# A one-core decoder layer: the expert routing list inverted by one-hot matmuls, rows gathered by the experts, residual and layernorm done on the sorted tiles

## The chip, the cores and the metric

The kernel runs on one core of a Trainium2 chip. The metric is device time in microseconds (us), the median of several executions. The core has a matrix engine (TensorE, PE in the rows), a vector engine (VectorE, DVE), an activation engine (ScalarE, ACT) and GpSimd (POOL). SyncE (SP) issues most DMAs; indirect DMAs, whose row numbers come from a table in memory, are issued by POOL.

## The reference, cut to what matters

The input is 32 batches of 128 tokens with 128 features, in float32. Three blocks follow each other, each with a residual and a layernorm. The change touches what surrounds the third, a mixture of eight experts with one expert per token:

```
x = layernorm(x + attention(x))                 # 16 heads, two segments
x = layernorm(x + cross_retention(x, ctx))      # x is called x2 from here on
gate_scores = softmax(x @ Wg + bg)              # 8 experts
e = argmax(gate_scores); top = gate_scores[e]
y = (silu(x @ W1[e] + b1[e]) @ W2[e] + b2[e]) * top
x = layernorm(x + y)
```

## The kernel before, in words

The kernel is five phases, one behind the other, each a block with its own program for every engine; the next block starts when all engines, and the DMAs they wait for, are done with the last one. The phases are `attention_phase`, `retention_phase`, `gate_phase`, `expert_phase` and `finish_phase`. Tokens lie as `[P, B, D]`: 128 token positions on the partitions, 32 batches, 128 features. Loops over groups of `G` = 4 batches give `NG` = 8 steps.

The retention phase works by groups and, on SP, loads the expert weights W1, W2 and the bias b2 ahead (`preload`). It then fills the DRAM buffer `sorted_x` from the tile `padding`: zero rows, each with a number of a spare output row.

The gate phase normalises x2 (`x2_row`), computes the logits, the softmax, `top` and the one-hot `hot`. Each expert's tokens are to fill whole tiles of 128 rows, so there are up to `NT` = 32 + 8 - 1 = 39 tiles. Two matmuls on `hot` and a chain of small DVE operations give, for each token, its row in the sorted order (`place`), and for each tile its expert (`tile_expert`). POOL then scatters x2 with 32 indirect DMAs, one per batch, into `sorted_x` (line 1142), the token's own number beside its 128 features.

The expert phase loads `sorted_x` back in four pieces (`cuts`). It runs over the 39 tiles in a loop of pairs. For tile t: ACT copies it (`e_x`), PE turns it (`e_turn`, line 1327), DVE evacuates it (`e_xT`, line 1414). Each engine reads the tile's expert number into a register (`expert_of`), and DVE copies that expert's W1 (`w_cur`, line 1410), ACT its biases (`b_cur`, line 1374). PE makes the hidden layer (`h_bank`, line 1343), ACT applies Silu (`hT`, line 1392), PE makes the output one tile later (`y_bank`, line 1353), DVE adds b2 (`y`, line 1433), and POOL scatters the tile's rows back into token order in the DRAM buffer `y_rows` (line 1314), behind a small addition (`carrier`, line 1313).

The finish phase loads `y_rows` in eight pieces, adds `y * top` to x2 and takes the statistics (DVE, partly POOL), makes mean and scale for all 32 batches at once (`norm_dve`, `norm_act`, lines 123 to 157), normalises and stores.

## Time and profile before

| | |
|---|---|
| time, median of 3 runs | 903.24 us (900.38 to 904.02) |
| the profiled execution | 903.15 us, span 901.3 us |
| busy share of the span | PE 79%, DVE 67%, ACT 59%, POOL 57% |
| granted TensorE clock, mean | 0.899 of 2.4 GHz |
| HBM traffic | 67.42 MB read, 43.16 MB written |

The span runs from the first to the last instruction of the profiled execution. Attention ends and retention begins at about 602 us, the gate phase begins at 684.8, the experts at 771.0 and the finish phase at 869.7. In the rows below a number in square brackets is the engine's idle time ahead of the instruction with what ended it. SPq stands for a DMA issue on SP's queue. The granted clock has two levels: 1.00 is 2.4 GHz, 0.50 is 1.2 GHz; a value between is a mean over a stretch in which it changed.

### The profile page before, as it was taken

The numbers are of one execution on the slowest core, as the hardware profiler recorded it, in microseconds if no ns is written. First come the engines' busy times: TensorE is split into PE (matmuls) and PEld (weight loads), VectorE is DVE, ScalarE is ACT, GpSimd is POOL, SyncE is SP. The second block draws the span as 40 slices with busy tenths as digits, with TensorE's granted clock in tenths as the row PEclk, the third lists the DMA queues.
The fourth block names the chain that finished last, engine by engine and source line by source line (L and its number), as shares of the span: only waits on it lengthen the run. The fifth ranks groups of instructions, "written<-read, shape, count | busy, mean of one in ns | idle before, by whom it ended". The sixth has DMA issues, their size and how long they took to land. (4 is left out here: it accounts for less than half of the span.)

```text
span 901.3 us, 26782 instructions
## 1 busy us (share of the span) xinstructions
PE 712.1 (79%) x9501; PEld 597.7 (66%) x9502; DVE 605.1 (67%) x1217; ACT 528.7 (59%) x1119; POOL 513.4 (57%) x524
## 2 busy tenths in 40 slices
PE   4789999999999999999999999748994600599920
PEld 3577788788778778778778877645664500598920
DVE  4378788788788788878878878745885510244438
ACT  3677787788788778778778878321221100477720
POOL 2167667757757756766765775633431167266742
PEclk8799999999999999999999999967996555699975
DMA  7567767767667677676776776611093011400033
GB/s 239 117 179 200 187 170 205 176 163 215 171 161 216 172 172 199 178 183 177 197 180 170 209 171 162 160 32 36 25 284 51 0 39 53 124 32 29 32 108 93
DMA packets 122154, 127.72 MB, mean 142 GB/s; under 512 B 7424, under 2 KB 101920, under 8 KB 118032
## 3 DMA queue, kind: packets, MB, share of 16 engines
q1 hardware_dynamic: 119584, 122.17, 52.8%
q0 software_dynamic: 2544, 5.21, 1.7%
q8 instruction: 15, 0.25, 0.1%
q14 instruction: 11, 0.09, 0.0%
HBM read 67.42 MB, written 43.16 MB: 123 GB/s over the span
## 5 line engine op out<-in xcount | busy, mean ns | idle before, releaser
L328 POOL TENSOR_TENSOR lhs<-pos_qv,ungate 64x1024 f32<-64x1024 f32 x64 | 151.7, 2370 | 161.9 <-PE mix L495 151.2
L614 ACT ACTIVATE psT<-bank 128x512 f32<-128x512 f32 x128 | 72.6, 594 | 92.5 <-PE bank L484 92.5
L766 DVE TENSOR_TENSOR lhs<-mix,zg_all 64x512 f32<-64x512 f32 x128 | 88.2, 689 | 5.8 <-PE mix L467 1.9
L353 POOL TENSOR_TENSOR e_qk<-e_qk 128x512 f32<-128x512 f32 (+2 forms) x96 | 78.6, 819 | 20.1 <-DVE e_qk L707 15.1
L484 PE MATMUL bank<-const,ps 128*128 128x128 f32 x512 | 70.0, 280 | 21.7 <-POOL ps L343 21.5
L598 ACT ACTIVATE e_qk<-e_qk 128x512 f32<-128x512 f32 x128 | 82.3, 643 | 0.0
L721 DVE TENSOR_REDUCE s_max<-bank 128x8 f32<-128x512 f32 x64 | 44.2, 691 | 48.7 <-PE bank L453 47.8
L467 PEld LDWEIGHTS mix<-pos_qv 64*64 64x64 f32 (+1 forms) x2048 | 65.6, 137 | 13.7 <-issue 11.2
L484 PEld LDWEIGHTS bank<-const,ps 128*128 128x128 f32 x512 | 55.2, 142 | 27.9 <-issue 15.7
L574 ACT ACTIVATE qk_tok<-bank 128x512 f32<-128x512 f32 x128 | 73.2, 601 | 0.0
L603 ACT ACTIVATE qkT<-bank 128x512 f32<-128x512 f32 x128 | 71.2, 610 | 1.8 <-PE bank L430 1.0
L467 PE MATMUL mix<-pos_qv 64*64 64x64 f32 (+1 forms) x2048 | 72.2, 225 | 0.0
L495 PE MATMUL mix<-psT,lhs 128*64 128x64 f32 x2048 | 69.7, 229 | 3.0 <-DVE lhs L766 2.2
L495 PEld LDWEIGHTS mix<-psT,lhs 128*64 128x64 f32 x2048 | 65.3, 143 | 8.6 <-issue 8.6
L389 PE MATMUL bank<-w_k,x_cur 128*128 128x512 f32 x192 | 63.6, 442 | 7.5 <-ACT psT L614 7.5
L430 PE MATMUL bank<-const,qk_tok 128*128 128x128 f32 x512 | 67.2, 273 | 2.7 <-DVE e_qk L707 2.1
L1410 DVE COPY w_cur<-w 128x512 f32 x39 | 16.8, 431 | 77.3 <-issue 48.6
L512 PE MATMUL bank<-w_o,attT 128*128 128x128 f32 x512 | 65.2, 282 | 4.0 <-DVE attT L700 4.0
L512 PEld LDWEIGHTS bank<-w_o,attT 128*128 128x128 f32 x512 | 61.0, 195 | 10.7 <-ACT qkT L603 7.1
L430 PEld LDWEIGHTS bank<-const,qk_tok 128*128 128x128 f32 x512 | 59.4, 140 | 12.8 <-DVE e_qk L707 2.5
L343 POOL TENSOR_TENSOR ps<-s_exp,row_rec 128x512 f32<-128x512 f32 x64 | 65.4, 1042 | 0.0
L336 POOL TENSOR_TENSOR ps<-pos_qv,sq_rec 128x1024 f32<-128x1024 f32 x32 | 60.9, 1902 | 5.9 <-POOL lhs L328 4.8
(212 smaller groups left out, 1694.5 us busy)
## 6 DMA issues: line engine op xcount, KB each, us to landing
scratch_qv<-qv_out SPq DMA_DIRECT2D x32, 1024.0 KB, 5.7
pos_qv<-scratch_qv SPq DMA_DIRECT2D x64, 512.0 KB, 6.6
swapT<-qkT SPq DMA_DIRECT2D x64, 256.0 KB, 4.0
zg_all<-scratch_z SPq DMA_DIRECT2D x64, 256.0 KB, 3.8
sorted_x<-padding SPq DMA_DIRECT2D x1, 2515.5 KB, 18.5
r_all<-in_x_dram SPq DMA_DIRECT2D x4, 512.0 KB, 7.0
cx<-in_ctx_dram SPq DMA_DIRECT2D x8, 256.0 KB, 2.7
w<-in_L_ffn_W_dram SPq DMA_DIRECT2D x1, 2048.0 KB, 9.7
```

Of the source, the lines that this page charges most:

```text
L328: pool.tensor_tensor(lhs[0:L, 1 - n, :, :], pos_qv[s, :, DK:], ungate[s, :, :], ALU.mult).then_inc(vg_ready, 1)
L353: pool.tensor_tensor(dst, e_qk[:, 0:c, DK:], e_qk[:, c:2 * c, DK:], ALU.add).then_inc(k_summed, 1)
L430: last = pe.transpose(qk_bank[f][:, i * P:(i + 1) * P], qk_tok[:, 4 * f + i, :], cst("ident"))
L467: last = pe.matmul(mix[odd * DK:(odd + 1) * DK, h // 8, at:at + DK], pos_qv[0:k, h, 0:DK], pos_qv[0:k, h, DK:], start=True, stop=True)
L484: last = pe.transpose(turn_bank[f % 2][:, i * P:(i + 1) * P], ps[:, 4 * f + i, :], cst("ident"))
L495: last = pe.matmul(mix[odd * DK:(odd + 1) * DK, n, at:at + L], lhs[:, 1 - n, h, :], psT[:, h, n * L:(n + 1) * L], start=True, stop=True)
L512: last = pe.matmul(score_bank[1][:, 0:D], attT[:, c, :], w_o[:, c, :], start=(c == 0), stop=(c == C // 2 - 1))
L574: act.activation(qk_tok[:, 8 * hh:8 * hh + 8, slot * DK:(slot + 1) * DK], half_bank(bank, hh), ACT.Copy).then_inc(evac, 1)
L598: act.activation(e, e, ACT.Exp, scale=-1.0).then_inc(grown, 1)
L603: act.activation(qkT[:, :, 4 * f:4 * f + 4], qk_bank[f][:, :].rearrange("p (c s) -> p s c", c=4), ACT.Copy).then_inc(qkT_evac, 1)
L614: act.activation(psT[:, 4 * f:4 * f + 4, :], turn_bank[f % 2][:, :].rearrange("p (h s) -> p h s", h=4), ACT.Copy).then_inc(psT_evac, 1)
L766: dve.tensor_tensor(dst, mix[odd * DK:(odd + 1) * DK, g, :].rearrange("p (i n k) -> p i n k", n=SEG, i=4), zg_all[odd * DK:(odd + 1) * DK, ...
```

## The change

The padding of `sorted_x` in the retention phase, the 32 scatters of the gate phase and the whole finish phase are gone. The gate phase now makes the inverse list, which token lies at each row of each tile. `place` is split into tile (shift by 7) and row in the tile (the low 7 bits). For each batch two one-hot matrices, `in_row` (128x128) and `in_tile` (128x39, multiplied by the token's number + 1 on POOL), are multiplied on PE and summed over the 32 batches in one bank. From the sum come `token_of` (the number, with 0 for empty rows) and `row_to` (the same, with a number past the end for empty rows). Meanwhile SP stores x2 with `top` in its last column to the DRAM buffer `x2_rows`.

In the expert phase POOL gathers each tile from `x2_rows` by `token_of` with one indirect DMA, the first 16 (`AHEAD`) at once and the others four at a time. The loops are written out: every engine's program is straight-line code over 39 tiles. PE turns the gathered tile directly. DVE adds b2, then in two more operations per tile makes the residual (`y * top + x2`) and its statistics; per group of four tiles it does `norm` (mean and variance) and one tile later `scale_of` (scale and shift). Between these, POOL raises the variance to -0.5 (`raise_var`). ACT normalises tile t - 6 in its step t, in place of the copy `e_x`. POOL scatters the finished tile straight to the output by `row_to`, with a bounds check that leaves the empty rows out. The functions `stage_w1`, `evac`, `hidden` and `output` do what the loop bodies did before. The diff, cut to its core:

```diff
+EMPTY = 2.0 * P * B
+AHEAD = 16
...
             for target, source in preload:
                 sp.dma_start(target, source).then_inc(preloaded, 16)
-            sp.wait_ge(padded, 2)
-            sp.dma_start(sorted_x.rearrange("(t p) d -> p t d", p=P), padding[:, :, :]).then_inc(preloaded, 16)
-            sp.wait_ge(preloaded, 16 * (len(preload) + 1))
+            sp.wait_ge(preloaded, 16 * len(preload))
...
-            pool.memset(padding[:, :, :], 0.0).then_inc(padded, 1)
-            pool.wait_ge(padded, 1)
-            pool.tensor_copy(padding[:, :, D:].rearrange("p t o -> p (t o)"), cst("spare_row")).then_inc(padded, 1)
...
+            sp.wait_ge(x2_kept, NG)
+            sp.wait_ge(top_kept, 1)
+            sp.dma_start(x2_rows.rearrange("(b p) d -> p b d", p=P), x2_row[:, :, :]).then_inc(x2_stored, 16)
+            sp.wait_ge(x2_stored, 16)
...
+            for b in range(B):
+                if b % G == 0:
+                    pe.wait_ge(in_row_ready, b // G + 1)
+                if b % (B // 2) == 0:
+                    pe.wait_ge(in_tile_ready, b // (B // 2) + 1)
+                last = pe.matmul(list_bank[:, 0:NT], in_row[:, b, :], in_tile[:, b, :], start=(b == 0), stop=(b == B - 1))
+            last.then_inc(listed, 1)
...
+            act.wait_ge(top_ready, 1)
+            act.activation(x2_row[:, :, D:].rearrange("p b o -> p (b o)"), top[:, :], ACT.Copy).then_inc(top_kept, 1)
...
-            pool.tensor_copy(x2_row[:, :, D:].rearrange("p b o -> p (b o)"), cst("token_row")).then_inc(x2_kept, 1)
-            pool.wait_ge(x2_kept, NG + 1)
-            pool.wait_ge(placed, 1)
-            for b in range(B):
-                pool.indirect_dma_start(sorted_x, bass.IndirectOffsetOnAxis(ap=place[:, b:b + 1], axis=0),
-                                        x2_row[:, b, :], None).then_inc(scattered, 16)
-            pool.wait_ge(scattered, 16 * B)
+            for i in range(2):
+                half_b = slice(i * B // 2, (i + 1) * B // 2)
+                dims = [P, B // 2, NT]
+                pool.wait_ge(placed, i + 1)
+                pool.tensor_tensor(in_tile[:, half_b, :], in_tile[:, half_b, :],
+                                   cst("token_row")[:, half_b].unsqueeze(2).to_broadcast(dims), ALU.mult).then_inc(in_tile_ready, 1)
...
-            dve.tensor_copy(place[:, :], place_f[:, :]).then_inc(placed, 1)
-def expert_phase(nc, const, w1, w2, biases, tile_expert, sorted_x, y_rows):
+            dve.tensor_copy(place[:, :], place_f[:, :]).then_inc(done, 1)
+            dve.wait_ge(done, n + 13)
+            dve.tensor_scalar(tile_u[:, :], place[:, :], 7, None, ALU.logical_shift_right).then_inc(done, 1)
+            dve.tensor_scalar(row_u[:, :], place[:, :], P - 1, None, ALU.bitwise_and).then_inc(done, 1)
+            dve.wait_ge(done, n + 15)
+            dve.tensor_copy(tile_f[:, :], tile_u[:, :]).then_inc(done, 1)
+            dve.wait_ge(done, n + 15)
+            dve.tensor_copy(row_f[:, :], row_u[:, :]).then_inc(done, 1)
+            dve.wait_ge(done, n + 17)
+            for g in range(NG):
+                if g % (NG // 2) == 0:
+                    s = slice(G * g, G * g + B // 2)
+                    dims = [P, B // 2, NT]
+                    dve.tensor_tensor(in_tile[:, s, :], cst("tile_at").unsqueeze(1).to_broadcast(dims),
+                                      tile_f[:, s].unsqueeze(2).to_broadcast(dims), ALU.is_equal).then_inc(placed, 1)
+                s = slice(G * g, G * g + G)
+                dve.tensor_tensor(in_row[:, s, :], cst("lane").unsqueeze(1).to_broadcast([P, G, P]),
+                                  row_f[:, s].unsqueeze(2).to_broadcast([P, G, P]), ALU.is_equal).then_inc(in_row_ready, 1)
+            dve.wait_ge(listed, 1)
+            dve.tensor_scalar(token_of[:, :], list_bank[:, 0:NT], -1.0, 0.0, ALU.add, ALU.max)
+            dve.tensor_scalar(empty[:, :], list_bank[:, 0:NT], 0.0, EMPTY, ALU.is_equal, ALU.mult).then_inc(done, 1)
+            dve.wait_ge(done, n + 18)
+            dve.scalar_tensor_tensor(row_to[:, :], list_bank[:, 0:NT], -1.0, empty[:, :], ALU.add, ALU.add)
...
+            def gather(t):
+                if t >= AHEAD + 4:
+                    pool.wait_ge(turned, t - AHEAD - 3)
+                pool.indirect_dma_start(xs[:, t, :], None, x2_rows,
+                                        bass.IndirectOffsetOnAxis(ap=token_of[:, t:t + 1], axis=0)).then_inc(x_loaded[t % (AHEAD + 4)], 16)
+            def scatter(t):
+                pool.wait_ge(scaled, t + 1)
+                pool.indirect_dma_start(y_rows, bass.IndirectOffsetOnAxis(ap=row_to[:, t:t + 1], axis=0), y[:, t, :], None,
+                                        bounds_check=P * B - 1, oob_is_err=False).then_inc(stored, 16)
+            def raise_var(g):
+                s = slice(G * g, min(G * g + G, NT))
+                pool.wait_ge(exponent, 1)
+                pool.wait_ge(var_ready, g + 1)
+                pool.tensor_tensor(power[:, s], var[:, s], minus_half[:, 0:s.stop - s.start], ALU.pow).then_inc(powered, 1)
+            pool.memset(minus_half[:, :], -0.5).then_inc(exponent, 1)
+            for t in range(AHEAD):
+                gather(t)
+            for t in range(0, NT, G):
+                raise_var(t // G)
+                for i in range(t, min(t + G, NT)):
+                    scatter(i)
+                for i in range(t + AHEAD, min(t + G + AHEAD, NT)):
+                    gather(i)
+            pool.wait_ge(stored, 16 * NT)
...
+                pe.transpose(turn_bank[t % 2][:, 0:P], xs[:, t, 0:D], ident).then_inc(turned, 1)
...
+            turn(0)
+            for t in range(NT + 1):
+                if t < NT:
+                    hidden(t)
+                if t + 1 < NT:
+                    turn(t + 1)
+                if t > 0:
+                    output(t - 1)
...
+            def stage_b(t):
+                p = t % 2
                 e = expert_of(act, t)
+                if t > 1:
                     act.wait_ge(y_added, t - 1)
...
+            def normalise(t):
+                act.wait_ge(normed, t // G + 1)
+                act.activation(y[:, t, :], y[:, t, :], ACT.Identity, scale=rstd[:, t:t + 1], bias=less[:, t:t + 1]).then_inc(scaled, 1)
+            stage_b(0)
+            for t in range(NT):
+                hidden(t)
+                if t + 1 < NT:
+                    stage_b(t + 1)
+                if t >= G + 2:
+                    normalise(t - G - 2)
+            for t in range(NT - G - 2, NT):
+                normalise(t)
...
+            def add(t):
+                dve.wait_ge(y_done, t + 1)
+                dve.tensor_tensor(y[:, t, :], y_bank[t % 2][:, 0:D], b_cur[t % 2][:, FT:], ALU.add).then_inc(y_added, 1)
+                dve.wait_ge(y_added, t + 1)
+                dve.scalar_tensor_tensor(y[:, t, :], y[:, t, :], xs[:, t, D:], xs[:, t, 0:D], ALU.mult, ALU.add).then_inc(y_kept, 1)
+                dve.wait_ge(y_kept, t + 1)
+                dve.bn_stats(stats[:, t, :], y[:, t, :]).then_inc(stats_done, 1)
+            def norm(g):
+                s = slice(G * g, min(G * g + G, NT))
+                at = 2 * g
+                def col(c):
+                    return stats[:, s, c:c + 1].rearrange("p b o -> p (b o)")
+                dve.wait_ge(stats_done, min(G * g + G, NT))
+                dve.tensor_tensor(mean[:, s], col(1), col(4), ALU.add)
+                dve.tensor_tensor(tmp[:, s], col(1), col(4), ALU.subtract)
+                dve.tensor_tensor(var[:, s], col(2), col(5), ALU.add).then_inc(chain, 1)
+                dve.wait_ge(chain, at + 1)
+                dve.tensor_scalar(mean[:, s], mean[:, s], 0.5, None, ALU.mult)
+                dve.tensor_scalar(var[:, s], var[:, s], 1.0 / D, EPS, ALU.mult, ALU.add)
+                dve.scalar_tensor_tensor(rstd[:, s], tmp[:, s], 0.25, tmp[:, s], ALU.mult, ALU.mult).then_inc(chain, 1)
+                dve.wait_ge(chain, at + 2)
+                dve.tensor_tensor(var[:, s], var[:, s], rstd[:, s], ALU.add).then_inc(var_ready, 1)
+            def scale_of(g):
+                s = slice(G * g, min(G * g + G, NT))
+                at = 4 * g
+                dve.wait_ge(powered, g + 1)
+                dve.tensor_tensor(tmp[:, s], power[:, s], power[:, s], ALU.mult).then_inc(polish, 1)
+                dve.wait_ge(polish, at + 1)
+                dve.tensor_tensor(tmp[:, s], tmp[:, s], var[:, s], ALU.mult).then_inc(polish, 1)
+                dve.wait_ge(polish, at + 2)
+                dve.tensor_scalar(tmp[:, s], tmp[:, s], -0.5, 1.5, ALU.mult, ALU.add).then_inc(polish, 1)
+                dve.wait_ge(polish, at + 3)
+                dve.tensor_tensor(rstd[:, s], power[:, s], tmp[:, s], ALU.mult).then_inc(polish, 1)
+                dve.wait_ge(polish, at + 4)
+                dve.scalar_tensor_tensor(less[:, s], mean[:, s], -1.0, rstd[:, s], ALU.mult, ALU.mult).then_inc(normed, 1)
+            stage_w1(0)
+            evac(0)
+            for t in range(NT + 1):
+                if t + 1 < NT:
+                    stage_w1(t + 1)
+                    evac(t + 1)
+                if t > 0:
+                    add(t - 1)
+                    if t % G == 0 or t == NT:
+                        norm((t - 1) // G)
+                    if t > G and t % G == 1:
+                        scale_of(t // G - 1)
+            scale_of(NT // G)
```

## Rows read from the trace of the kernel before

**Rows 1.** By stretch: length, busy of PE, PEld, DVE, ACT, POOL; clock; DMA.
```profile
684.80:725.10 40.30, 22.55 (x101) 21.02 (x101) 24.58 (x90) 6.70 (x11) 5.14 (x9) 0.50 0.01 1
725.10:771.00 45.90, 0.00 (x0) 0.00 (x0) 0.04 (x1) 0.00 (x0) 31.07 (x32) 0.50 0.14 46
771.00:869.60 98.60, 82.76 (x664) 78.45 (x664) 36.77 (x118) 66.21 (x236) 57.30 (x118) 0.93 0.18 52
869.60:901.30 31.70, 0.00 (x0) 0.00 (x0) 25.31 (x96) 1.51 (x2) 8.01 (x8) 0.50 0.46 133
```

**Rows 2.** The padding store (KB, us to landing; when issued) and the gate's beginning.
```profile
sorted_x<-padding SPq DMA_DIRECT2D x1, 2515.5 KB, 18.5
...
L874 SPq DMA_DIRECT2D sorted_x<-padding x1: 1698/1698/1698, 665.9 to 665.9; - x1
...
684.90 0.21 DVE L137 TENSOR_TENSOR g_mean<-stats 128x32 f32<-128x32 f32 x1 [4.30 <-PEq L816]
```

**Rows 3.** From the list to the experts: timeline, and the scatters' tile view.
```profile
724.96 0.18 DVE L1247 CAST place<-place_f 128x32 uint32<-128x32 f32 x1
726.02 1.08 POOL L1142 DMA_INDIRECT sorted_x<-x_row,place  x1 [19.91 <-DVE place L1247]
...
L1142 POOL DMA_INDIRECT sorted_x<-x_row,place x32: 963/967/1082, 726.0 to 765.6; - x32
...
771.00 3.97 SPq L1291 DMA_DIRECT2D xs<-sorted_x  x4
```

**Rows 4.** Timeline: the nearest operations to the list's on DVE, POOL and PE.
```profile
656.90 0.69 DVE L1024 TENSOR_TENSOR k_cos<-r_k,const 128x512 f32<-128x512 f32 x1 [0.17 <-PE r_k L938]
...
656.82 1.27 POOL L894 TENSOR_TENSOR qh<-q_cos,q_sin 128x512 f32<-128x512 f32 x1 [3.48 <-DVE q_sin L1024]
...
706.71 3.42 PE L1102 MATMUL g_logit<-wg,x2T 128*128 128x8 f32 x16
```

**Rows 5.** Timeline of one tile in the experts' loop, at full clock.
```profile
806.11 0.29 DVE L1433 TENSOR_TENSOR y<-y_bank,b_cur 128x128 f32<-128x128 f32 x1 [0.49 <-PE y_bank L1353]
806.53 0.31 ACT L1374 ACTIVATE b_cur<-biases 128x132 f32 x1 [0.44 <-DVE y L1433]
806.55 0.19 POOL L1313 TENSOR_TENSOR carrier<-xs 128x1 f32<-128x1 f32 x1 [0.52 <-DVE y L1433]
...
807.15 0.43 DVE L1410 COPY w_cur<-w 128x512 f32 x1 [0.75 <-PE h_bank_b L1343]
807.20 1.25 POOL L1314 DMA_INDIRECT y_rows<-y,row  x1 [0.46 <-DMA y_rows<-y,row]
...
809.08 0.99 POOL L1314 DMA_INDIRECT y_rows<-y,row  x1 [0.17 <-issue]
```

**Rows 6.** Timeline of the first tiles, written out and at half clock.
```profile
777.28 0.29 DVE L1414 COPY e_xT<-e_turn 128x128 f32<-128x128 f32 x1 [1.56 <-PE e_turn L1327]
...
778.03 0.43 DVE L1410 COPY w_cur<-w 128x512 f32 x1 [0.46 <-issue]
...
781.62 0.29 DVE L1433 TENSOR_TENSOR y<-y_bank,b_cur 128x128 f32<-128x128 f32 x1 [1.32 <-PE y_bank L1353]
```

**Rows 7.** Timeline: small DVE operations of the layernorms.
```profile
685.79 0.19 DVE L145 TENSOR_TENSOR g_var<-g_var,g_rstd 128x32 f32<-128x32 f32 x1
...
890.43 0.19 DVE L150 TENSOR_TENSOR o_tmp<-o_rstd 128x32 f32<-128x32 f32 x1
890.66 0.19 DVE L152 TENSOR_TENSOR o_tmp<-o_tmp,o_var 128x32 f32<-128x32 f32 x1
```

**Rows 8.** PE's last and first matmuls about pauses, and the granted clock.
```profile
860.00 2.30 PE L1353 MATMUL y_bank<-w,hT 128*128 x16
...
866.00:868.00 2.00, 0.00 (x0) 0.00 (x0) 0.00 (x0) 0.00 (x0) 0.00 (x0) 0.67 0.00 0
...
774.03 0.48 PE L1327 MATMUL e_turn<-const,e_x 128*128 128x128 f32 x1 [56.27 <-ACT e_x L1367]
...
781.00:782.00 1.00, 1.00 (x10) 1.00 (x9) 0.29 (x1) 0.00 (x0) 0.00 (x0) 0.82 0.30 70
```

301 lines of the change are left out of this document (82 added, 219 removed).

## The prediction

> **What bounds the kernel now.** I read the stages first, from the busy time by stretch [rows 1]. TensorE (PE) is the busiest engine only while the experts run (82.8 of 98.6 us). From 725.1 to 771.0 POOL alone is busy (31.1 of 45.9 us), and from 869.6 to the end DVE is (25.3 of 31.7 us). The change touches these 216 us and one wait ahead of them, so a gain or a loss has to be found stage by stage. In the timeline DVE waits 4.30 us before its first instruction of the gate stage, and the store of `padding`, issued at 665.9 and landed 18.5 us later (684.4), is what ends then [rows 2]. The scatters into `sorted_x` are 32 indirect DMAs whose first and last start lie 39.6 us apart, 1.28 us each; behind the last one SP starts only at 771.00, 4.4 us after its end [rows 3].
>
> **Ahead of the experts.** Removed: the padding store. The next thing that ends is DVE's own work (680.6), plus the handover of 0.5 us seen behind the store (684.4 to 684.90): 3.8 us gained [rows 2]. The weights' preloads stand ahead of the store in SP's queue, and I take them to have landed by then. Removed too: everything from the end of `place` (725.14) to 771.00, 45.9 us [rows 3]. In its place:
> - four small DVE operations, 0.6 us by the 0.18 us of `place` [rows 3];
> - one `in_tile` of 128x624: DVE takes 0.69 us for 512 elements, so 0.84 [rows 4];
> - POOL's multiply of it: 1.27 us for 512, so 1.55, and 0.1 for the handover [rows 4]. Its second half, and the `in_row` groups (0.69 us each against four matmuls each), lie beside the matmuls;
> - 32 matmuls of 128x39. Sixteen records (8 fp32 matmuls of 8 columns) took 3.42 us, 0.43 each [rows 4], at the granted clock 0.50 of the whole stage [rows 1], so 1.2 GHz. The weight load sets this, so 39 columns cost the same: 13.7 us. At full clock it would be half, 6.9; I take the slow value, since the clock never rose in this stage;
> - three DVE operations and the handover, 1.2 us.
>
> Sum 18.0 us, for 45.9. The store of `x2_rows` is 2,064 KB; at 18.5 us for 2,515 KB it takes 15.2 us, and even if issued only at 725 it lands before the list is ready at 743. So the experts start 27.9 + 3.8 = 31.7 us earlier.
>
> **The experts, and a ring of waits.** The finish stage is gone: experts plus finish take 901.3 - 771.0 = 130.3 us now. The new stage must stay below 130.3 + 31.7 = 162.0 us to break even. What sets it is the order on POOL: `raise_var(g)`, four scatters, four gathers, `raise_var(g+1)`. Scatter 4g+3 waits for ACT's `normalise(4g+3)`, which ACT does in its step 4g+9, behind `stage_b(4g+10)`, which waits for `y_added` of tile 4g+8. DVE adds that tile in its step 4g+9 and then stands at `scale_of(g+1)`, which needs `raise_var(g+1)`. So a scatter, four gathers and the power lie between two DVE instructions, once per group. Behind the waiting DVE are `stage_w1` and `evac` of the next tile, so PE and ACT run dry too. One turn, from `scale_of(g)` to `scale_of(g+1)`:
> - DVE: `scale_of`, five dependent operations 0.22 us apart, 1.08 [rows 7]; `norm`, 684.90 to 685.98, 1.08 [rows 2, 7]. A tile: 0.46 for the register load, 0.43 for `w_cur`, 0.29 for `e_xT` [rows 6], then the add, the residual and the statistics, 3 x 0.32 with their waits, by the 0.29 of `y` [rows 5]: 2.14 us. Three tiles, then the front of a fourth up to `y_added` (1.50). 1.08 + 6.42 + 1.08 + 1.50 = 10.1.
> - ACT: 0.13 to `b_cur`, 0.31 for it [rows 5], and the same again for `normalise`: 0.8.
> - POOL: 0.88 from release to the start of an indirect DMA (725.14 to 726.02) and five of them at 1.28 [rows 3]; the power by the smallest operation there, `carrier`, 0.19 [rows 5]; less the last pitch's gap, with handovers: 7.3.
>
> At full clock this is 18.2 us. But DVE stands still for 7.5 us, and PE has nothing from about 2.4 us after the last `evac` until `scale_of` and the next tile's load, copy and `evac` are through: 8.3 us idle. Before the change PE ended at 862.30 and the clock had fallen by 868 (0.67 over 866 to 868) [rows 8]. After a pause PE began at 774.03 and the clock came back only in 781 to 782 (0.82) [rows 8]. So the clock falls in each turn and the next tiles run at 1.2 GHz. There, from the end of an `e_xT` (777.57) to the `y` behind it (781.62) take 4.05 us [rows 6], where DVE's own work would have filled 2.14. The second tile of a turn is late by 1.9, the third by up to 1.5 more. I add 2.6, between 1.9 and 3.4: 20.8 us.
>
> The Trainium skill ("TensorE: Matmul & The Clock Gate", section on HAM oscillation) describes a kernel whose waits for data cool the array in every iteration, so that each begins at the low rate. By that rule every turn here would be cold; if the rule did not bite, the sum would be the 18.2 us turn. The fall behind 862.30 agrees with it.
>
> **Sum.** Start: `y` of tile 0 at 10.6 us into the stage, as before (781.62 - 771.00) [rows 6], since the first gather takes the place of the first load; four tiles more at 2.3, one `norm` and an add give 21.8. POOL's 16 gathers end at 21.2, about together. Then turns: five with four gathers (104.0), one with three (19.5), two with none. These are shorter by 5.1: 15.7 cold or 13.1 warm, and since PE idles only 3.2 us in them I take 14.4 (28.8). Tail: `scale_of(8)`, four scatters, `raise_var(9)`, `scale_of(9)`, three normalisations, three scatters: 14.1, and 4.4 us for the end behind an indirect DMA [rows 3]: 18.5. Total 21.8 + 152.3 + 18.5 = 192.6, against 162.0: 30.6 us slower. The profiled execution took 903.15 us (span 901.3), within 0.1 us of the median 903.24. 903.2 + 30.6 gives 933.8, and I say 933.
>
> **Unknown costs.** The gather's time on POOL and the bounds check of the scatter have no row. The nearest is 1.28; the loop of before shows 1.25 with 0.46 ahead, 1.71 [rows 5], and without any gap it would be 0.97. 54 of them are on the path, so -17 to +23 us. The power: 0.19 to the 1.27 of POOL's 128x512 [rows 4, 5], nine times, up to +10. The list at full clock: -6.8. That `Identity` makes ACT reload its table I exclude, since `Copy` between two `Silu` doesn't now.
>
> The slow 1.25 us DMA began at 807.20, beside DVE's copy `w_cur` from 807.15; others take 0.99 [rows 5]. The Trainium skill ("SBUF — State Buffer", Door table and its warning on software DMA) says that such a copy locks GpSimd out of writing descriptors. It speaks against a change that doubles these DMAs; the row's 0.25 us agrees, but the gathers run while DVE waits, so by the rule too the sum barely moves.
>
> **Rivals.**
> - *The clock stays up* (the pauses are shorter than I think): turns of 18.2, 16.9 and 13.1 us, 134.1 in all, stage 174.4, time 915.6. For it: one fall only in a comparable place. Chance 0.14.
> - *Indirect DMAs or the power dearer* (1.71 us each): 957. Chance 0.10.
> - *Faster: the ring doesn't close.* If POOL reaches `raise_var` before DVE needs it, turns last DVE's 4 x 2.14 + 2.16 = 10.7 us (POOL's own 8 x 1.28 + 0.3 is as long): 21.8 + 8 x 10.7 + 18.5 = 125.9, 36 us less than now, 867. It decides once a turn is below (162.0 - 40.3) / 8 = 15.2 us on average, where I have 19.0. Against it: the order of the queues as printed. Chance 0.10, with all that ends faster.
> - *It comes out even*: turns between, 0.05.
>
> **Numbers.** The forecast (920 to 950) has 0.61. The range 908 to 957 holds it, the warm clock and the bound of 1.71 us. About 0.5% (4.5 us) can be told from no change. Faster 0.10, same 0.05, slower 0.85.
>
> **What would show it.** DVE's `scale_of` waits about 7 us for POOL in groups 1 to 5 and about 2 us later; gathers start 16 early and then four per turn; the stage from its first gather to the end lasts about 193 us; the granted clock alternates in it; the list takes 14 us and the gate ends near 739. It is wrong if `scale_of` doesn't wait, or if a gather holds POOL for far less than 1.28 us.

## The result and the profile after

The changed kernel takes 948.04 us (median of 4 runs, 946.16 to 949.78) where the one before, run beside it, takes 903.63. The ratio is 1.0497, with a 95% interval from 1.0464 to 1.0531: 5.0% slower. The forecast was 933 us, with a range of 908 to 957. The profiled execution took 947.7 us, its span is 945.7.

By stretch, as [rows 1] before (length, busy time of PE, PEld, DVE, ACT, POOL, granted clock, DMA share, GB/s). The stretches are the gate phase up to `place`, the list, the experts up to the first `scale_of`, from there to `scale_of(8)`, and the tail:

```profile
679.44:719.72 40.28, 22.55 (x101) 21.02 (x101) 24.65 (x91) 6.96 (x12) 4.96 (x8) 0.51 0.32 50
719.72:737.65 17.93, 13.85 (x64) 13.73 (x64) 9.45 (x17) 0.00 (x0) 3.23 (x3) 0.50 0.07 9
737.65:771.40 33.75, 17.40 (x101) 16.18 (x102) 9.95 (x36) 10.76 (x33) 16.64 (x18) 0.69 0.15 32
771.40:923.76 152.36, 84.42 (x564) 79.37 (x562) 63.03 (x257) 57.91 (x196) 62.51 (x63) 0.78 0.10 23
923.76:945.70 21.94, 0.00 (x0) 0.00 (x0) 4.09 (x23) 2.91 (x7) 7.84 (x8) 0.55 0.03 9
```

No engine is busy for even six tenths of the 152 us in the middle. The stage from 737.65 to the end lasts 208.05 us; experts and finish lasted 130.3 before.

Ahead of the experts the timeline answers to [rows 2, 3, 4]. The wait of 4.30 us before the gate phase's first instruction is 0.31 now. The list is made of the operations that the prediction named:

```profile
679.44 0.21 DVE L139 TENSOR_TENSOR g_mean<-stats 128x32 f32<-128x32 f32 x1 [0.31 <-PEq L818]
...
720.32 0.81 DVE L1273 TENSOR_TENSOR in_tile<-const,tile_f 128x624 f32<-128x624 f32 x1
721.21 1.61 POOL L1156 TENSOR_TENSOR in_tile<-in_tile,const 128x624 f32<-128x624 f32 x1 [20.74 <-DVE in_tile L1273]
722.96 13.85 PE L1121 MATMUL list_bank<-in_tile,in_row 128*128 128x39 f32 x64 [10.67 <-POOL in_tile L1156]
...
737.18 0.20 DVE L1282 SCALAR_TENSOR_TENSOR row_to<-list_bank,empty 128x39 uint32<-128x39 f32 x1
737.65 0.10 POOL L1341 MEMSET minus_half<- 128x4 f32 x1 [10.67 <-POOLq L1033]
```

In the middle of the experts, POOL's timeline shows one turn of the ring in the order in which it is queued: the last of four scatters, four gathers, the power. DVE's row, from the start of this turn, shows who stands behind it (the one at its end, 831.11, has the same wait):

```profile
823.95 0.97 POOL L1331 DMA_INDIRECT out_dram<-y,row_to  x1 [2.26 <-ACT y L1417]
825.22 1.00 POOL L1326 DMA_INDIRECT xs<-x_rows,token_of  x1 [0.30 <-issue]
826.52 0.97 POOL L1326 DMA_INDIRECT xs<-x_rows,token_of  x1 [0.30 <-issue]
827.79 0.95 POOL L1326 DMA_INDIRECT xs<-x_rows,token_of  x1 [0.30 <-issue]
829.05 0.95 POOL L1326 DMA_INDIRECT xs<-x_rows,token_of  x1 [0.30 <-issue]
830.02 1.05 POOL L1339 TENSOR_TENSOR e_power<-e_var,minus_half 128x4 f32<-128x4 f32 x1
...
810.53 0.16 DVE L1476 TENSOR_TENSOR e_tmp<-e_power 128x4 f32<-128x4 f32 x1 [8.05 <-POOL e_power L1339]
```

The first instructions of `scale_of` start at 771.40, 789.97, 810.53, 831.11, 851.67, 872.17, 891.43, 907.32, 923.76 and 931.89: turns of 18.6, then four of 20.5 to 20.6, 19.3, and two of 15.9 and 16.4. The wait of 8.05 us stands before each full one. The windows of the turn from 809.5 to 830 show the clock: half while the first tiles run, full for the rest of the work, and fallen again before the pause is over.

```profile
809.50:816.00 6.50, 3.19 (x15) 3.22 (x16) 3.01 (x12) 1.95 (x6) 2.05 (x2) 0.50 0.06 13
816.00:818.00 2.00, 2.00 (x17) 2.00 (x17) 0.94 (x3) 0.77 (x3) 0.00 (x0) 0.82 0.10 33
818.00:826.00 8.00, 5.14 (x41) 4.50 (x39) 3.94 (x17) 4.41 (x16) 3.70 (x4) 1.00 0.07 23
826.00:828.00 2.00, 0.00 (x0) 0.00 (x0) 0.00 (x0) 0.00 (x0) 1.39 (x3) 0.74 0.14 33
828.00:830.00 2.00, 0.00 (x0) 0.00 (x0) 0.00 (x0) 0.00 (x0) 1.69 (x2) 0.50 0.31 66
```

One thing was not in the prediction. The opening, from the stage's first instruction to the first `scale_of`, takes 33.75 us and not 21.8. Its timeline has two stalls in which nobody but POOL works:

```profile
749.56 1.06 PE L1379 MATMUL y_bank<-w,hT 128*128 x8
...
753.21 0.29 DVE L1444 TENSOR_TENSOR y<-y_bank,b_cur 128x128 f32<-128x128 f32 x1 [5.72 <-remote]
...
759.56 0.63 ACT L1412 ACTIVATE hT<-h_bank_a,b_cur 128x128 f32<-128x128 f32 x2 [5.62 <-remote]
...
761.06 0.29 DVE L1440 COPY e_xT<-e_turn 128x128 f32<-128x128 f32 x1 [5.96 <-remote]
...
761.46 1.84 PE L1368 MATMUL h_bank_b<-e_xT,w_cur 128*128 128x128 f32 x7 [10.84 <-issue]
```

"Remote" stands where the semaphore waited for rose well after any recorded work that could have raised it. PE's records say that it was done with tile 1 at 750.6; ACT goes on at 759.6 and DVE at 761.1. All this time POOL issues gathers: 39 of them take 37.8 us, 16 stand in an unbroken string from 738.43 to about 758, 1.26 us apart.

### The profile page after: what moved, and what is told of

Read it like the earlier page. It is cut to its first block and busy times, and to the rows that moved or that the text cites. A ratio compares the mean times of both kernels' runs of the same rounds, so it can differ in the third digit from the quotient of the medians.

```text
span 945.7 us, 26226 instructions
## 1 busy us (share of the span) xinstructions
PE 744.7 (79%) x9564; PEld 629.0 (67%) x9564; DVE 628.1 (66%) x1334; ACT 533.3 (56%) x1116; POOL 502.2 (53%) x454
## 5 line engine op out<-in xcount | busy, mean ns | idle before, releaser
L486 PE MATMUL bank<-const,ps 128*128 128x128 f32 x512 | 71.5, 284 | 21.6 <-POOL ps L345 21.3
L1331 POOL DMA_INDIRECT out_dram<-y,row_to x39 | 38.8, 994 | 89.6 <-ACT y L1417 86.1
L1368 PE MATMUL h_bank_b<-e_xT,w_cur 128*128 128x128 f32 x152 | 29.6, 356 | 70.4 <-DVE w_cur L1436 58.9
L1400 ACT ACTIVATE b_cur<-biases 128x132 f32 x39 | 12.2, 313 | 128.6 <-DVE y L1444 92.0
L1368 PEld LDWEIGHTS h_bank_b<-e_xT,w_cur 128*128 128x128 f32 x152 | 25.7, 256 | 73.4 <-DVE w_cur L1436 61.5
L514 PEld LDWEIGHTS bank<-w_o,attT 128*128 128x128 f32 x512 | 61.3, 196 | 10.6 <-ACT qkT L605 7.0
```

The lines of the kernel that those rows point to most:

```text
L486: last = pe.transpose(turn_bank[f % 2][:, i * P:(i + 1) * P], ps[:, 4 * f + i, :], cst("ident"))
L514: last = pe.matmul(score_bank[1][:, 0:D], attT[:, c, :], w_o[:, c, :], start=(c == 0), stop=(c == C // 2 - 1))
L1368: last = pe.matmul(h_bank[p][part][:, f * P:(f + 1) * P], w1_cur[p][:, f * P:(f + 1) * P], xT[p][:, :], start=True, stop=True)
```

## The experiments

There are twelve runs, on three chips, each with the kernel before beside it: beside the first four it took 900.07 us, beside the second four 900.92, then 900.33 (the first probe and all gathers first) and 901.31 (the second probe and the paced gathers). By its ratio of 1.0497 the kernel after would take 944.8 to 946.1 there. So sizes of a few us are compared by the length of the stage in each run's own trace, from the first POOL instruction of the experts' block to the end (208.1 us in the kernel after), and by its parts: the opening (to the first `scale_of`, 33.8), the turns (from one `scale_of` to the next) and the tail. Against the kernel before a version breaks even where the stage takes 130.3 + 27.9 + 4.0 = 162.2 us.

**The power a scatter earlier.** This opens the ring in one place: the last scatter of a group no longer stands in POOL's queue ahead of the power for which DVE waits, and the four gathers behind it don't either.

```diff
+            raise_var(0)
             for t in range(0, NT, G):
-                raise_var(t // G)
                 for i in range(t, min(t + G, NT)):
+                    if i == t + G - 1 and t + G < NT:
+                        raise_var(t // G + 1)
                     scatter(i)
```

> The changed kernel with one reordering on POOL: raise_var(g+1) stands between scatter 4g+2 and scatter 4g+3 instead of behind the four gathers; no work is added or removed. Theory (the ring through POOL sets the turn): scale_of no longer waits for the gathers, a turn falls from 20.6 us to what POOL needs for itself, 8 indirect DMAs at 1.27 us plus 1.05 us for the power and its handovers, 11.4 us, and to 10.1 us (DVE's own) where there are no gathers: about 64 us less, 884 us. Rival (a turn is long because of the amount of work, the cold clock or PE): the same instructions on every engine, so no change, 948 us.

Measured 905.75 us (ratio to before 1.0047, 1.0029 to 1.0065). The stage takes 168.5 us, 39.6 less than in the kernel after. DVE's wait for the power, 57.5 us in 9 in the kernel after, is gone (2.3). So the ring is real: opened in this one place it gives back 39.6 of the 45.9 us by which the stage exceeds the break-even length. But of the turns only the first (10.8) and the last full one (10.6) are short, and in neither is a gather issued (the first one behind the opening starts at 781.33, the last at 861.87); the others are 14.1 to 16.5, and the time expected was 884. DVE's groups of this run show what came in its place (line, operation, tiles, count, busy and mean ns, idle before and its releasers):

```profile
L1446 DVE TENSOR_TENSOR y<-y_bank,b_cur 128x128 f32<-128x128 f32 x39 | 11.2, 286 | 25.4 <-PE y_bank L1381 13.5 <-remote 10.8 <-issue 1.1
L1442 DVE COPY e_xT<-e_turn 128x128 f32<-128x128 f32 x39 | 11.1, 284 | 24.5 <-remote 18.9 <-PE e_turn L1360 4.6 <-issue 1.0
```

**The clock kept up.** PE gets dummy matmuls of the identity in each pause.

```diff
+                for _ in range({10: 36, 14: 36, 18: 36, 22: 36, 26: 36, 30: 36, 34: 14}.get(t, 0)):
+                    pe.matmul(turn_bank[t % 2][:, P:2 * P], ident, ident, start=True, stop=True)
```

> The changed kernel with idle matmuls (128x128, identity by identity, into an unused part of a PSUM bank) at the end of PE's step in each turn, 36 in the six turns with gathers and 14 in the next, so that PE is busy while DVE waits for POOL. Theory (the pause lets the clock fall, and the cold tile costs about 2.1 us per turn: y of the second tile at 816.8 where DVE was ready at 814.7): the granted clock stays at 1.00, each of seven turns is about 2.1 us shorter, 15 us less, 933 us. Rival (the cold clock is hidden by the ring): clock up, time unchanged within 3 us.

Measured 933.31 us (931.01 to 934.09), the number expected, but the kernel after would take 944.8 here: the gain is 11.5 us by the times and 12.8 by the stage (195.3 us), and 15 were expected. The granted clock is 1.00 through all eight turns, and DVE's wait before `scale_of` stays at 8.1 us in the full ones. The full turns are 18.8 to 19.2 instead of 20.6. The cold clock costs about 1.7 us in each turn of four gathers and over 2 in the short ones.

**No gathers.** SP loads whole tiles of unsorted rows, everything else stays.

```diff
             def gather(t):
-                if t >= AHEAD + 4:
-                    pool.wait_ge(turned, t - AHEAD - 3)
-                pool.indirect_dma_start(xs[:, t, :], None, x2_rows,
-                                        bass.IndirectOffsetOnAxis(ap=token_of[:, t:t + 1], axis=0)).then_inc(x_loaded[t % (AHEAD + 4)], 16)
+                pass
...
+        @block.sync
+        def _(sp):
+            for t in range(NT):
+                if t >= AHEAD + 4:
+                    sp.wait_ge(turned, t - AHEAD - 3)
+                b = t % B
+                sp.dma_start(xs[:, t, :], x2_rows[b * P:(b + 1) * P, :]).then_inc(x_loaded[t % (AHEAD + 4)], 16)
```

> The changed kernel with POOL's gathers left out: SP loads whole unsorted tiles of x2_rows with one plain DMA each instead, so the rows are not routed and the output is another. The scatters and the power stay on POOL. Theory (the gathers lie inside the ring, 4 x 1.27 us per turn): six turns shrink by 5.1 us to about 16, 29 us less. For the two stalls of about 6 us on DVE and ACT early in the expert stage (748 to 753 and 755 to 761), which no wait explains: if POOL's string of 16 gathers holds them up, they vanish too (11 us more, about 909 us); if they come from loading the written-out programs alone, they stay (about 920 us).

Measured 898.38 us (ratio to before 0.9975, 0.9943 to 1.0007). Both branches of the expectation were too high. The opening is 19.1 us and no "remote" is left in DVE's groups:

```profile
L1449 DVE TENSOR_TENSOR y<-y_bank,b_cur 128x128 f32<-128x128 f32 x39 | 11.1, 284 | 12.0 <-PE y_bank L1384 11.9
L1445 DVE COPY e_xT<-e_turn 128x128 f32<-128x128 f32 x39 | 11.1, 283 | 7.7 <-PE e_turn L1363 7.7
```

The ring stays closed here, but with the scatter and the power alone in it: turns of 13.7 to 16.5. The stage takes 161.2 us, which is the break-even length. So the gathers take 46.9 us of the kernel after: 14.7 in the opening, 29.1 in the turns, where four of them lie in the ring, and 3.1 in the tail. The 39 loads carry as many rows of 516 bytes into the same tiles, so it isn't the bytes.

**Twelve gathers ahead instead of sixteen.**

```diff
-AHEAD = 16
+AHEAD = 12
```

> The changed kernel with 12 gathers ahead instead of 16. In the ring there are then 27 gathers instead of 23, 5.1 us more. If the two early stalls on DVE and ACT end with POOL's opening string of gathers (16 of them end at 758.5, the stall at about 760), the string is 5.1 us shorter and the first scale_of comes about 5 us earlier: no change in all, 948 us. If they come from loading the programs alone, they last as long and the time is 5 us longer, 953 us.

Measured 944.18 us (941.07 to 946.52). The opening is 29.0 us, 4.8 shorter than with 16. Four gathers less are 5.0 us less of string. But four more gathers now lie in the turns (five of 20.6 to 20.9, one of 19.3 where there was one of 15.9), and these are 5.0 us longer together. The stage is 208.3 us: all given back. The 0.7 us by which the time is below 944.8 is less than the runs differ among themselves.

**The list alone.** This is one half of the change: the list and the gathers stay, the scatters go to `y_rows` unnormalised, and the finish phase of before follows.

```diff
             for t in range(NT + 1):
                 ...
                 if t > 0:
                     add(t - 1)
-                    if t % G == 0 or t == NT:
-                        norm((t - 1) // G)
-                    if t > G and t % G == 1:
-                        scale_of(t // G - 1)
...
-            for t in range(0, NT, G):
-                raise_var(t // G)
-                for i in range(t, min(t + G, NT)):
-                    scatter(i)
-                for i in range(t + AHEAD, min(t + G + AHEAD, NT)):
-                    gather(i)
+            for t in range(NT):
+                scatter(t)
+                if t + AHEAD < NT:
+                    gather(t + AHEAD)
...
+        finish_phase(nc, r_all, x2_row, stats, top, y_rows, out)
```

> One half of the change alone: the list by one-hot matmuls and the experts' gathers stay, but each y tile is scattered unnormalised to y_rows as soon as it is added, and residual and layernorm are done in the finish stage of before. There is no ring: no POOL instruction stands between two DVE instructions. By my theory (the ring of waits is what makes the change slow, the list is a gain of 31.7 us): experts start at about 737, last about 99 us as before plus the late PE signals beside gathers (12 us in the opening, some more later), finish 31.7: 870 to 890 us, clearly below before. Rival (gathers and scatters on POOL as such are what costs): POOL has 78 indirect DMAs at about 1.27 us = 99 us, on top of the late signals, so the experts last 120 us or more and it ends at 895 or above.

Measured 906.5 us (ratio 1.0057, 1.0031 to 1.0082). My theory of that point, that only the ring stands against the list's gain of 31.7 us, fails: without any ring the kernel is no faster than before. The rival's number holds but not its reason, since POOL is far from full (77 us of 139). The windows of this run, from its first gather, show where the time is:

```profile
736.75:762.00 25.25, 8.24 (x44) 7.41 (x44) 3.08 (x9) 5.98 (x16) 17.45 (x18) 0.64 0.20 47
762.00:840.00 78.00, 57.21 (x399) 54.86 (x400) 22.86 (x71) 34.39 (x116) 45.08 (x45) 0.84 0.15 37
840.00:862.00 22.00, 22.00 (x197) 21.83 (x196) 10.82 (x35) 16.78 (x59) 11.29 (x12) 1.00 0.10 34
862.00:875.67 13.67, 3.29 (x28) 2.91 (x26) 0.88 (x3) 1.90 (x7) 3.49 (x4) 0.76 0.02 4
```

While gathers run, PE is busy 0.33 and 0.73 of the time. From 840 on only scatters remain, and PE is busy without a gap, at full clock, a tile in 1.9 us. The experts last 138.9 us where before they lasted 98.6. Of the 40 us, 3 lie behind the last scatter (see the drain below); the other 37, by subtraction, are lost while gathers run.

**Gathers and scatters in turn.** The version with the early power, with each gather behind one scatter in place of four together.

```diff
                     scatter(i)
-                for i in range(t + AHEAD, min(t + G + AHEAD, NT)):
-                    gather(i)
+                    if i + AHEAD < NT:
+                        gather(i + AHEAD)
```

> raise_var ahead of the fourth scatter, as in the run with the early power, and in addition each gather follows one scatter in place of four gathers in a row. If PE's signals come late because gathers are issued in an unbroken string, these stalls (19.7 us of ACT waits for hT in the early-power run) fall by half or more and the turns go from 15.4 to 13.5 or so: 890 us. If each gather holds a signal up by itself, wherever it stands, nothing changes: 905.

Measured 896.28 us (ratio 0.9939, 0.9914 to 0.9964), between the two expectations. The turns are 13.6 to 13.8 as the first one said, but the opening keeps its 33.8 us. The stage takes 158.0 us, 4.2 below the break-even length. It is the first version that beats the kernel before, by 0.6%.

**A multiply for the power.**

```diff
-                pool.tensor_tensor(power[:, s], var[:, s], minus_half[:, 0:s.stop - s.start], ALU.pow).then_inc(powered, 1)
+                pool.tensor_tensor(power[:, s], var[:, s], minus_half[:, 0:s.stop - s.start], ALU.mult).then_inc(powered, 1)
```

> The kernel after with a multiply in place of the power in raise_var (so the values scaled by are not the right ones); everything else as it is. The power took 1.05 us in the trace of after; a multiply of 128x4 should take about 0.2. If the power is on the ring, each of the nine turns gets about 0.85 us shorter: 940.5 us, 7.7 less than after. If it is hidden, 948.

Measured 940.44 us (938.62 to 941.55), the number expected, but partly by luck: the kernel after would take 945.7 on this chip, so that 938 would have been the number, and the stage is 203.8 us, only 4.3 shorter. POOL's rows show that the operation itself is 0.83 us cheaper and DVE's wait for it 7.5 us shorter in all:

```profile
L1339 POOL TENSOR_TENSOR e_power<-e_var,minus_half x10: 203/215/229, 767.8 to 925.5; 128x4 f32<-128x4 f32 x9, 128x3 f32<-128x3 f32 x1
...
  DVE e_tmp L1476: 50.0, 9
```

The full turns are 20.4 instead of 20.6. In the turn from 810.5 in the kernel after and the one from 807.8 here, PE's first group of eight `h_bank_a` matmuls took 1.12 us there and 1.86 here: in this turn the clock came back later in the work, which took back 0.74 us. The other turns I did not compare. So of the 0.83 us that the power costs more in each of ten groups, which lies on the ring, about half reached the end.

**Gathers of one element.** The kernel without gathers, with gathers put back that fetch 4 bytes a row into a tile that nobody reads.

```diff
             def gather(t):
+                pool.indirect_dma_start(junk[:, t, :], None, x2_rows.rearrange("r (d o) -> (r d) o", o=1), ...).then_inc(junked, 16)
```

> The run without gathers (SP loads unsorted tiles, so the output is another one) with gathers put back that fetch one element per row in place of 129, into a tile that nobody reads, in the places of the gathers of after. If what makes PE's signals late is that POOL writes descriptors (128 a gather, whatever they carry), the long opening comes back: from the stage's first instruction to the first scale_of 29 to 34 us, as in after (33.75), against 19.1 without gathers, and turns near 20. If it is the bytes that are moved, or what waits for the gathered data, the opening is limited by POOL's issue alone: the power can't start before 16 gathers at 1.27 us are through, 21 to 24 us, and no wait for a late signal shows.

Measured 942.96 us in a single execution, with a stage of 206.5. The opening is 32.1 us and the full turns 20.6 to 21.3: nearly the whole loss comes back though no engine waits for the data of these gathers and they carry 1/129 of it. In the turns that follows from their place alone, since they stand in POOL's queue ahead of the power. In the opening it doesn't: 16 gathers take POOL 20 us, and the opening lasts 12 us longer. So a gather costs what an indirect DMA of 128 rows costs, whatever it moves.

**A probe of independent strings.** Ahead of its experts' work PE runs 192 small matmuls and ACT 78 small copies, which wait for nothing, beside the opening gathers.

```diff
+            for i in range(192):
+                last = pe.matmul(turn_bank[1][:, P:2 * P], ident, ident, start=True, stop=True)
+                if i % 8 == 7:
+                    last.then_inc(probe_pe, 1)
...
+            for i in range(2 * NT):
+                act.activation(y[:, i // 2, D // 2 * (i % 2):D // 2 * (i % 2 + 1)], ident[:, 0:D // 2], ACT.Copy).then_inc(probe_act, 1)
```

> A measurement inside the list-alone kernel. At the start of the experts' block PE first runs 192 matmuls of 128x128 that depend on nothing, each eighth of which raises a semaphore, and ACT runs 78 copies of 128x64, each of which raises one, while POOL issues its 16 opening gathers (20 us) and then stands still. If a gather holds up PE itself (or its signals) and not a wait between the engines, the semaphore of PE's string rises rarely in the 20 us of the gathers (8 matmuls should take about 1.8 us at 1.2 GHz and 0.9 or less at 2.4) and evenly behind them; ACT's stays even all the time if only PE is touched. If instead what was late is one engine waiting for another by way of the gathered data, both strings run evenly from the first matmul on.

Timeline of this run (one execution, 951.27 us, taken for its trace), gathers from 736.80 to 756.8:

```profile
736.08 8.87 ACT L1409 ACTIVATE y<-const 128x64 f32<-128x64 f32 x60 [29.37 <-PEq L1033]
736.11 9.60 PE L1374 MATMUL e_turn<-const 128*128 128x128 f32 x65 [0.88 <-PEq L1033]
...
745.28 0.98 ACT L1409 ACTIVATE y<-const 128x64 f32<-128x64 f32 x5 [0.33 <-issue]
...
750.28 0.39 PE L1374 MATMUL e_turn<-const 128*128 128x128 f32 x2 [1.73 <-issue]
...
752.40 0.56 PE L1374 MATMUL e_turn<-const 128*128 128x128 f32 x1 [1.73 <-issue]
...
755.81 0.95 POOL L1325 DMA_INDIRECT xs<-x_rows,token_of  x1 [0.30 <-issue]
...
759.43 10.79 PE L1374 MATMUL e_turn<-const 128*128 128x128 f32 x74 [0.34 <-issue]
```

Both strings run at full pace for 9 us (ACT 60 copies, 0.146 apart) and then crawl together: in the 14.2 us from 745.2 to 759.4 PE has 13 matmul records (two for each float32 matmul), and ACT needs 7.8 us, 745.28 to 753.06, for its last 18 copies. They come singly or in groups of up to five that stand 0.70 us or a multiple apart. At 759.43, 3.6 us after the last gather's issue, PE is back at its pace. So PE isn't waiting for another engine, and it isn't PE alone: the expectation's branch "ACT's stays even" fell. Only the profile's "late signals" of PE had made it look so.

**The same probe with few, long instructions.**

```diff
+            for i in range(48):
+                pe.matmul(h_bank[1][1][:, :], ident, const[:, 0:BANK], start=True, stop=True).then_inc(probe_pe, 1)
...
+            for i in range(36):
+                if i >= 9:
+                    act.wait_ge(probe_act, i - 8)
+                act.activation(y[:, 4 * (i % 9):4 * (i % 9) + 4, :].rearrange("p t d -> p (t d)"), const[:, 0:BANK], ACT.Copy).then_inc(probe_act, 1)
```

> The probe again with few, long instructions in place of many short ones: PE runs 48 matmuls of 128x512 that depend on nothing, ACT 36 copies of 128x512, each raising a semaphore, beside the 16 opening gathers. In the first probe both strings kept their pace for 8.4 us (65 matmuls with their weight loads, 60 copies) and then crawled together, with starts 0.7 us or a multiple apart, until the last gather had landed. If what is held up is the supply or the recording of instructions, one by one, these strings, with a quarter of the instructions, run through the whole 20 us of the gathers at an even pace (about 0.85 us a matmul at the slow clock, 0.43 at the fast one, 0.6 us a copy). If it is the engines' reads and writes of their memories, or time since the gathers began, they crawl from about 8 us on as before.

Timeline of this run (one execution, 939.02 us) up to 762, with the same 16 gathers from 738.74 to 758.7:

```profile
738.02 18.81 ACT L1409 ACTIVATE y<-const 128x512 f32<-128x512 f32 x36 [29.35 <-PEq L1033]
738.04 24.25 PE L1374 MATMUL h_bank_b<-const 128*128 128x512 f32 x51 [0.88 <-PEq L1033]
738.74 1.09 POOL L1325 DMA_INDIRECT xs<-x_rows,token_of  x1 [11.40 <-SPq L1288]
...
757.71 0.95 POOL L1325 DMA_INDIRECT xs<-x_rows,token_of  x1 [0.31 <-issue]
```

No gap in either: copies start 0.52 us apart through all of it, matmul records 0.43 apart once the clock is up (PE's string goes on to 781.6, 96 records in all). The gathers don't touch how fast PE and ACT compute or read. They hold up the passing of single instructions. Whether what counts is the rate of these or their number, this run doesn't tell: up to the end of the gathers it has only 43 matmul records and 36 copies, where the first probe got 65 and 60 through before it slowed.

**All gathers first**, in the list-alone kernel.

```diff
-            for t in range(AHEAD):
+            for t in range(NT):
                 gather(t)
             for t in range(NT):
                 scatter(t)
-                if t + AHEAD < NT:
-                    gather(t + AHEAD)
```

> The list-alone kernel with all 39 gathers issued before the first scatter. They take 49 us on POOL (1.26 each). If PE stands still for about as long as gathers are being issued (39 gathers cost about 40 us in the list-alone run, wherever they stood), PE gets some 5 tiles done in these 49 us and the other 34 at 1.9 us each as in the stretch of that run without gathers: experts 49 + 65 + 13 = 127 us where the list-alone run had 139, 895 us in all. If PE gets nothing at all done in a dense string: 903. If the cost was the exchange of gathers and scatters on POOL and not the gathers as such, PE runs at 2.3 us a tile from the start and the kernel ends at 880 or below.

Measured 908.23 us (ratio 1.0082, 1.0056 to 1.0108), worse than either of the readings gave that held gathers to be the cause. Windows of this run:

```profile
738.00:787.00 49.00, 12.66 (x61) 11.56 (x61) 4.28 (x12) 6.29 (x17) 36.38 (x39) 0.60 0.22 50
787.00:800.00 13.00, 3.22 (x15) 3.25 (x16) 1.21 (x4) 2.82 (x9) 3.92 (x4) 0.50 0.22 28
800.00:860.00 60.00, 59.99 (x531) 59.62 (x531) 28.63 (x93) 44.91 (x155) 30.07 (x31) 0.99 0.10 31
```

PE gets 61 matmul records through in the 49 us of gathers, and only 15 in the 13 us behind them. All 15 come after 796.78:

```profile
796.78 0.55 PE L1354 MATMUL h_bank_a<-e_xT,w_cur 128*128 128x128 f32 x1 [33.85 <-issue]
```

So the stall outlasts the last gather, which ends at 787.9, by 8.9 us, two scatters among them. Behind a string of 16 gathers it was 3.0 us in the kernel after (758.5 to 761.46) and 2.7 in the first probe, behind 12 it was 2.4. The longer the string, the longer the time until PE is back, as if something were still being worked off. DVE stands too, once for 17.9 us with no releaser. From 800 on PE runs without a gap beside 31 scatters. Scatters 1.9 us apart do no harm; what they do in an unbroken string beside PE no run shows.

**Paced gathers.** The interleaved version, meant to have 8 gathers in a row in the opening and 8 that each wait for PE.

```diff
             for t in range(AHEAD):
+                if t == 12:
+                    raise_var(0)
+                if t >= 8:
+                    pool.wait_ge(turned, t - 7)
                 gather(t)
```

> The interleaved version (896.3 us) with the opening gathers paced as well: only 8 in a row, the other 8 each wait until PE has taken the tile seven before, and raise_var(0) stands after the twelfth. If an unbroken string of gathers is what stops PE (1 or 2 tiles in 17 us in the opening), the first scale_of comes about 8 us earlier and the kernel ends near 888. If each gather costs PE about 1 us wherever it stands, nothing is gained: 896.

Measured 896.72 us (ratio 0.9946, 0.9916 to 0.9976), the same as without pacing. The opening is 27.4 us in place of 33.8, the full turns behind it are 13.9 to 16.3 in place of 13.7, and the stage is 158.4 us in place of 158.0: given back one for one. The edit paces less than the expectation says. By POOL's rows 11 gathers still stand in an unbroken string (735.11 to 748.7), since PE had already taken the tiles for which the ninth to eleventh wait; the twelfth follows at 750.92 and the last four in a row from 761.02, behind the power. So this run shows a shorter string and not the absence of one.

## Why the prediction was right, point by point

The direction, the ring and the time ahead of the experts were as written. The forecast of 933 us is 15 short of the measured 948. The stage is 15.5 us longer than the 192.6 of the sum, and that sits in two terms, the opening and the tail.

- **Ahead of the experts.** The padding store: 4.0 us (the wait fell from 4.30 to 0.31), 3.8 predicted. The list: 17.9 us, 18.0 predicted, at the clock of 0.50. The store of `x2_rows`, issued at 708.38, is hidden. The first instruction of the stage comes at 737.65, 1.7 us ahead of the 739.3 that follow from the prediction, of which the retention phase, which ended earlier in this execution, gives 1.5.
- **The ring.** Predicted were waits of about 7 us before `scale_of`, turns of 20.8 and 19.5 and 152.3 us for eight turns. Measured: waits of 8.05, turns of 20.5 to 20.6 and 19.3, and 152.36. That the sum fits to 0.1 us is partly luck: the first turn is 18.6, the short ones are 15.9 and 16.4 where I took 14.4, and the POOL part is made up otherwise. From the start of the last scatter (823.95) to the end of the power (831.07) are 7.1 us, predicted 7.3, but with a power of 1.05 in place of 0.19 and without the 0.88 us that I had put ahead of the first DMA. The run with the early power shows the ring itself (39.6 us of the stage), the run with the multiply the power's share (4.3).
- **The clock.** Taken as 2.6 us a turn. The granted clock is 0.50 for the first 6 us of each full turn, and the dummy matmuls give back 1.7 in a full one, 12.8 us in all (the 18 that the rival put on it was too much). A turn at full clock is 18.8 and not 18.2: that the cold one comes to the 20.8 of the sum within 0.3 is two errors that cancel. The rival with a clock that stays up fell. The rule cited from the Trainium skill ("TensorE: Matmul & The Clock Gate", HAM oscillation), that waits for data cool the array in every iteration, agrees with the windows shown above.
- **Mis-sized: the opening.** "`y` of tile 0 at 10.6 us into the stage ... give 21.8" was 33.75. That term took the engines' own pace as free of POOL's work. In the run without gathers it is 19.1, so the whole excess of 12.0 us comes with the string of 16 gathers. The prediction had only asked when POOL would be done with them (21.2), and put at nothing what they do to the other engines.
- **Mis-sized: the tail.** 18.5 predicted, 21.9 measured. The last scatter starts at 936.78 and the span ends 8 us after its end, where the 4.4 us behind an indirect DMA of [rows 3] had been taken; that difference of 3.6 is the whole of it. What fills the time is POOL's drain at the end of its block. Its rows, first of the kernel after (78 indirect DMAs in the block), then of the run without gathers (39):

```profile
L1288 POOLq DRAIN  x1: 6439/6439/6439, 939.0 to 939.0; - x1
```

```profile
L1288 POOLq DRAIN  x1: 3243/3243/3243, 890.8 to 890.8; - x1
```

  In the trace of before the same instruction takes 2.68 us behind the 32 scatters, and 3.23 behind the 39 of the experts. So it is 0.083 us for each indirect DMA of the block, 3.2 us for the 39 gathers.
- **The unknown costs.** An indirect DMA is 0.96 us and 1.27 apart, as the nearest row said, gathers and bounds-checked scatters alike. The row of 1.25 us in [rows 5] has a counterpart: of the 78 in the kernel after one is slow, the scatter at 835.14 with 1.21 us, which starts 0.13 us behind a `w_cur` copy, and in the run with the early power one at 801.06 takes 1.22, 0.08 us behind such a copy. The gathers beside DVE's copies in the opening last 0.95 us as those do in the pauses. So the locked-port rule of the Trainium skill ("SBUF — State Buffer", Door table and its warning on software DMA) agrees with a quarter of a microsecond in single rows, and as predicted the sum doesn't feel it.
- **The rival that ends faster** had the right lever and the wrong price. With the ring opened the turns should have been 10.7 us and the time 867; they were mostly 14 to 16.5 and the time 905.8. The cost that stands behind, gathers against the instructions of PE and ACT, wasn't in any of the rivals. By the prediction one moved line would have turned the loss into a gain of 36 us. It only gives the loss back, and gathers and scatters in turn bring the 0.6%.

## What to carry to other kernels

Look for an instruction on a slow queue that stands between two instructions of an engine on which the others wait (here DVE): one line moved there (`raise_var` before the fourth scatter) was worth 39.6 us. When work moves to another engine's queue, write down that queue's order for one full period and ask who waits behind each entry. Before building on many indirect DMAs beside short instructions, run a string of independent work beside them: in the list-alone version the engines lost some 37 us while 39 gathers ran, and gathers whose data nobody wanted brought back 13.0 of the 14.7 us that the opening gains without any.

## What the runs showed of the hardware

- While POOL issues gathers back to back, instructions of PE and ACT pass in steps of 0.70 us, mostly one to three at a time (13 matmul records in 14.2 us, 18 copies in 7.8), after about 9 us at full pace. It goes on behind the last gather, 2.4 to 3.0 us after 12 or 16 of them and 8.9 after 39. Long instructions pass undisturbed. Loads of as many rows by SP do nothing of the kind, gathers of 4 bytes a row do nearly all of it.
- The cause is only narrowed down. Either the engines' supply of instructions is held up, or the recording of them: every execution timed here was also recorded, so that the recorder can't be told from the chip. On the supply the Trainium skill ("Runtime: NRT & Kernel Launch", Instruction fetch mechanics) says that each sequencer fetches its instructions by a DMA queue of its own. The traces list such transfers, and they speak against a late one. In the run with all gathers first PE stands from 762.9 to 796.78, and from 760 to 797 the only DMA traffic is that of the indirect DMAs; the next instruction transfers come at 798.3 and 798.7, when PE is already back. The queues of the stretches 760 to 797 and 797 to 800:

```profile
q0 software_dynamic: 810, 1.66, 23.1%
```

```profile
q0 software_dynamic: 32, 0.07, 7.7%
q8 instruction: 1, 0.02, 2.0%
q14 instruction: 1, 0.01, 0.6%
```

  The first probe has none from 746 to 773 either, while its crawl begins at 745 and ends at 759. The profile doesn't say which engines the two queues serve, so this doesn't close the question.
- The records themselves suffer beside the gathers, even where the engines don't. In the second probe each copy of ACT from the tenth on waits for the one nine before it, and all 36 run 0.52 us apart, so that the signals came in time; yet the trace has a semaphore event for only 19 of them. Of PE's 48 signals there 41 are in the trace, ten up to 757.93 and then seven within 0.25 us from 761.43. In the first probe 61 of ACT's 78 are there, with gaps from 739 us on, and the last stands at 758.69, where the last copy ended at 753.3. So part of what the profile calls "remote" can be late records. Whether the recording also holds up the engines isn't shown. The Trainium skill ("NOTIFIC — Programmer's Manual", When the ring fills) says that a record queue can be set to stall its producer, and that dropping the record that doesn't fit is the default. Missing records agree with dropping, from which standing engines wouldn't follow; no run here tells how the queues were set. A timing of the kernel with all recording off would decide.
- POOL takes 1.05 us for a power of 128x4 and 0.215 for a multiply of it.
- The drain that ends POOL's block takes 0.083 us for each indirect DMA that the block issued (2.68, 3.23 and 6.44 us for 32, 39 and 78).
